# GpSimd's products with B issued three steps ahead of their scans in place of two, in a selective-scan kernel on one core

## The reference

```python
dt = softplus(einsum('blr,dr->bld', dt, dt_proj_w) + dt_proj_b)
A = -exp(A_log)
def step(h, inputs):
    dt_t, B_t, C_t, u_t = inputs
    dA = exp(dt_t[:, :, None] * A)
    h = dA * h + (dt_t * u_t)[:, :, None] * B_t[:, None, :]
    y = einsum('bdn,bn->bd', h, C_t)
    return (h, y)
...
y = ys.transpose(1, 0, 2) + u * D
y = y * silu(z)
```

## Time and profile before

| | us |
|---|---|
| median of 3 runs | 1285.89 |
| lowest, highest | 1283.64, 1287.6 |
| the profiled execution | 1284.42 |
| its span, first to last instruction | 1282.6 |

### The profile page before, as it was taken

How to read it: one execution, slowest core, us unless ns; L and a number is a source line. 1 busy time by engine, 2 the same in 40 slices (tenths; PEclk the granted TensorE clock), 3 DMA queues, 4 the chain that set the end, 5 groups by cost and what they waited for, 6 DMA issues and landing times.

```text
span 1282.6 us, 13041 instructions
## 1 busy us (share of the span) xinstructions
PE 1072.5 (84%) x3642; PEld 613.6 (48%) x3642; DVE 1150.1 (90%) x1341; ACT 819.0 (64%) x1532; POOL 1106.9 (86%) x747
## 2 busy tenths in 40 slices
PE   5678878888888887888888889888878878888797
PEld 4334545545545544544455455445445445454344
DVE  1299999999999999999999999999999999999782
ACT  2476766766666667757667666666667676576543
POOL 4199898898898898998988988988988989989663
PEclk8699998998998999999999989989999999998898
DMA  6222221221222312212222212222122132222561
GB/s 162 76 76 76 81 100 65 98 100 58 99 76 86 101 57 105 100 57 98 87 77 80 101 57 99 93 71 99 59 102 101 57 105 100 74 99 87 181 206 37
DMA packets 64538, 116.78 MB, mean 91 GB/s; under 512 B 34218, under 2 KB 47954, under 8 KB 64466
## 3 DMA queue, kind: packets, MB, share of 16 engines
q1 hardware_dynamic: 64466, 115.96, 26.9%
HBM read 108.47 MB, written 7.47 MB: 90 GB/s over the span
## 4 chain that ended last, share of the span: by engine, by line
POOL 27%; DVE 24%; issue 21%; PE 19%; ACT 7%; POOLq 0%; DMA 0%; DVEq 0%; SPq 0%; ACTq 0%
POOL SCAN L414 15%; DVE SCAN L984 15%; PE Yp L711 7%; POOL SCAN L426 6%; DVE SCAN L939 5%; PE PP L740 2%; PE PP L862 2%; PE PP L790 2%; PE PP L842 2%; POOL XN L451 2%; PE PP L835 1%; DVE GATES L968 1%; ACT SGZ L599 1%; POOL GATES L419 1%; POOL XN L442 1%
## 5 line engine op out<-in xcount | busy, mean ns | idle before, releaser
L984 DVE TENSOR_TENSOR_SCAN SCAN<-DA,CAR,SCAN 128x384 f32<-128x384 f32 x768 | 729.8, 1000 | 39.3 <-POOL SCAN L426 35.7
L414 POOL TENSOR_TENSOR SCAN<-SCAN,CS 128x768 f32<-128x768 f32 x384 | 692.3, 1817 | 23.1 <-DVE SCAN L984 18.9
L711 PE MATMUL Yp<-SCAN,IDENT 128*128 128x384 f32 x1536 | 592.6, 511 | 101.1 <-POOL SCAN L414 93.0
L491 ACT ACTIVATE DA<-UDT,A 128x384 f32<-128x384 f32 x768 | 441.6, 581 | 365.3 <-DVE SCAN L984 362.5
L711 PEld LDWEIGHTS Yp<-SCAN,IDENT 128*128 128x128 f32 x1536 | 288.8, 198 | 309.8 <-POOL SCAN L414 147.3
L939 DVE TENSOR_TENSOR SCAN<-UDT,BB 128x768 f32<-128x768 f32 x288 | 268.4, 932 | 11.1 <-PE BB L693 9.2
L426 POOL TENSOR_TENSOR SCAN<-UDT,BS 128x768 f32<-128x768 f32 x96 | 174.4, 1817 | 0.0
L862 PE MATMUL PP<-XN,WT 128*128 128x384 f32 x384 | 140.4, 501 | 0.0
L446 POOL TENSOR_TENSOR UDT<-UDT 128x768 f32<-128x768 f32 x24 | 43.5, 1811 | 69.9 <-DVE UDT L1068 69.9
L862 PEld LDWEIGHTS PP<-XN,WT 128*128 128x128 f32 x384 | 75.6, 199 | 56.7 <-issue 11.7
L693 PE MATMUL BB<-PT,SEL 96*128 96x384 bf16 x288 | 97.7, 340 | 4.1 <-DVE SCAN L939 4.1
(11 more groups left out here) (167 smaller groups left out, 1090.2 us busy)
## 6 DMA issues: line engine op xcount, KB each, us to landing
CS<-bc_rows SPq DMA_DIRECT2D x96, 768.0 KB, 4.1
BS<-bc_rows SPq DMA_DIRECT2D x24, 768.0 KB, 6.0
out<-XN SPq DMA_DIRECT2D x32, 192.0 KB, 2.5
X<-in_x SPq DMA_DIRECT2D x24, 192.0 KB, 3.5
X<-in_L_ffn_memory_tokens SPq DMA_DIRECT2D x16, 256.0 KB, 3.0
XN<-in_L_ffn_memory_tokens SPq DMA_DIRECT2D x16, 256.0 KB, 3.3
bc_rows<-XDT SPq DMA_DIRECT2D x24, 48.0 KB, 1.5
X<-in_L_ffn_memory_router SPq DMA_DIRECT2D x1, 512.0 KB, 4.0
```

Source lines behind the costliest of these rows:

```text
L414: pool.tensor_tensor(M[:, n1 % MRING], HB[:, n1 % HRING], over_halves(CS[:, n1 % CRING]), ALU.mult).then_inc(m_ready, 1)
L491: act.activation(DA[:, h, 0:T], DT[:, par, h], ACT.Exp, scale=A[:, h, n:n + 1])\
L711: last = pe.matmul(Yp[:, h, 0:T], IDENT[:, :], M[:, n3 % MRING, h], start=n3 == 0, stop=n3 == NS - 1)
L984: dve.tensor_tensor_scan(HB[:, s % HRING, h], DA[:, h, 0:T], HB[:, s % HRING, h], CAR[:, ds(J * NS * HALVES + s * HALVES + h, 1)], ALU.mul ...
```

## The change

GpSimd's `step` issues the product with B for state s + 3 where it issued it for state s + 2. The states 3, 5, 7 and 9 so get their product in the steps 0, 2, 4 and 6 in place of 1, 3, 5 and 7. The wait for `car_saved` follows n2 and stays what it was for each state.

```diff
--- before.py
+++ after.py
-                if main and s + 2 in POOL_STATES:
+                if main and s + 3 in POOL_STATES:
-
-                    n2 = s + 2
+
+                    n2 = s + 3
                     pool.wait_ge(bs_loaded, 16 * (J + 1))
                     pool.wait_ge(dtu_ready, J + 1)
                     pool.wait_ge(car_saved, 4 * BATCH + 4 * J + (n2 - HRING) // GRP + 1)
```

## The result

| | before | after |
|---|---|---|
| median, us | 1286.09 (4 runs, 1283.64 to 1287.6) | 1314.72 (4 runs, 1313.2 to 1317.12) |
| ratio to before | | 1.0226, interval 1.0202 to 1.025 |
| span of the profiled execution, us | 1282.6 | 1314.2 |

The change makes the kernel slower by 28.6 us, 2.3%. The direction was forecast; the forecast loss was 15.4 us, and the time lies 2.7 us above the forecast range.

The account below looks back on a forecast made before the run. No engine is full; a unit is bound by a ring of GpSimd from DTU to B(9) and VectorE from scan 9 to the next DT. 20 units x 0.72 plus 1 us gave +15.4, 1285.9 to 1301.3 us; range 1284 to 1312.

Parts of the forecast that it names:

- The waits for B go: VectorE's waits before scans 3, 5 and 9 for GpSimd's products with B all vanish: minus 1.76 us a unit.
- GZ, +1.39: GpSimd's GZ, one slot later, makes VectorE's VV, ahead of drive(4), U and scan 3, start 1.39 us later.
- BB(10) and the means, +0.72 together: On TensorE, M4 one slot later delays BB(10) and the means, so VectorE's scan 10 starts 0.72 us later each unit.
- M(10)'s wait: GpSimd's wait for scan 10 ahead of M(10) grows from 0.32 to about 1.0 us.
- No collision of the moved products with VectorE, and L968 as before: Large VectorE operations in steps 0 to 6 read PSUM, so moved products collide with nothing; L968 keeps its anchors.
- The step that failed: Later BB(6), BB(8) and output projection on TensorE fall into 1.7 us of room before M4; costed at nothing.
- Unit 0 loses nothing: The first unit has no GZ and no VV, so it was to lose nothing.
- The units 21 and 22: Fewer means or a VV that comes late anyway: 1 us of loss together, an estimate.
- The rival of the clock: TensorE's 1.2 GHz stretch reaches past M4, costing another 1.4 us a unit: 1315 us for half, 1329 for all; chance 0.09.
- TensorE catches up: Rival: the chain from Yp(4) has unseen cover, only GZ binds, minus 7.4 us, 1278.5 us; chance 0.10.
- the race at L968 turns: Rival: VectorE reaches L968 ahead of GpSimd's product in each unit, saving 1.56 us, 1270 us; chance 0.05.

Follow-up runs that it names:

- fill_both: The changed kernel with 17 unused matmuls on TensorE ahead of Yp(0) and 7 ahead of Yp(4); 1299.91 us, 1.0104 to before.
- a_fill: The changed kernel with 20 unused matmuls on TensorE ahead of Yp(0); 1317.81 us, 1.0255 to before.
- b3_back: The changed kernel with only B(3) put back to two steps ahead, where it was before; 1317.21 us, 1.0239 to before.
- v_b579: Kernel before with B(5), B(7), B(9) a step earlier; TensorE's means ahead of Yp(6), dt projection, BB(10) and D product ahead of Yp(4); 1297.89 us.
- b7_back: The changed kernel with only B(7) put back to two steps ahead, behind M(4); 1314.48 us, 1.0217 to before.
- b3_only: The kernel before with only B(3) moved to three steps ahead; 1315.15 us, 1.0224 to before.
- v_all: The changed kernel with TensorE's means ahead of Yp(6), and dt projection, BB(10) and product with D ahead of Yp(4); 1316.22 us, 1.0222 to before.
- v_pe: Kernel before, products with B unmoved; TensorE's means ahead of Yp(6), dt projection, BB(10) and product with D ahead of Yp(4); 1295.68 us, 1.007.
- b_fill: The kernel before with 12 unused matmuls on TensorE ahead of Yp(0); 1285.19 us, 1.0001 to before.

## Why the prediction was right in sign and short in size

- *The waits for B go*: right. No scan of the units 1 to 20 waits for L426.
- *GZ, +1.39*: right, 1.36 in the timeline, 25.8 us in 19 waits.
- *BB(10) and the means, +0.72 together*: right at full clock, and only there. `fill_both` shows drive(10) waiting 0.92 (0.75 forecast), XC 0.31 (0.35 to 0.45), scan 10 late by 0.73, a unit of 50.40, M(10)'s wait at 20.7 us in 20 (1.0 forecast) and 1299.91 us for 1301.3. In after itself none of these is the binding wait: drive(10) doesn't wait, drive(6) does.
- *No collision of the moved products with VectorE, and L968 as before*: right. M in steps 0 to 6 kept 1.8 us a piece, L968 its 2.5.
- *The step that failed*: "BB(6), BB(8) and the output projection then fall into the 1.7 us that TensorE has before M4 [...] I cost these at nothing; if that cover is gone, a late BB(6) costs some tenths, and drive(10)'s wait of 0.75 swallows them." The term was put at nothing, and it measured 1.16 us a unit. The working, from the rows: BB(6) had 2.22 us ahead of drive(6) before, 0.14 of which the start of drive(6) takes, and VectorE comes there 1.39 - 0.32 = 1.07 later, so BB(6) could be 3.15 us late for nothing. Yp(0) is 1.77 us later, which that cover holds. But from the start of Yp(0) to the end of BB(6) it is 5.81 us in after (576.96 to 582.77) against 3.19 in before (611.15 to 614.34), 2.62 more at the low clock: 4.39 late in all, 1.24 beyond the cover, and drive(6) waits 1.16. Yp(1) adds another 0.3. The 1.7 us ahead of M(4) were gone as well, and drive(10) had no wait left that could have swallowed the late BB(6). With the low clock a unit loses 1.51 us where the sum had 0.72: 0.79 a unit, 15.8 us over twenty units, against the 13.2 us by which the medians miss the forecast.
- *Unit 0 loses nothing*: not so. At the first operation behind L419 of unit 1 (GZ at 110.83 before, B(3) at 112.17 after) after is 1.3 us late, 0.4 of it from ahead of unit 0. The units 21 and 22 lost 1.1 us for a forecast of 1.
- *The rival of the clock* was named, with a price that came out near the result (1315 for half of the units), at 0.09 and for the wrong reason. That the number is near is luck. I let the clock count only if the low stretch reached past M(4), and held against it that the low stretches of before ended with the x projection. In after they reach into Yp(1) and no further; that is enough, because BB(6), which VectorE waits for, stands in them. I priced the steps behind the longer idle stretch with full-clock durations. The rows of the units 1 to 20 of before alone would not have given the loss either: Yp(0) or the x projection was slow in 12 of them, but the low clock added only 1.3 to 1.7 us a unit (2.93 and 1.71 us in unit 12), about half of the 3.2 us in after, and with that BB(6) comes out just in time on paper. The row that had it was the earlier trace rows, which I read only for the 0.14 us: it is BB(6) of unit 22 and drive(6) waiting 0.40 for it, behind 3.40 us of idle, a Yp(0) of 2.90 us and an x projection of 2.77. With these durations BB(6) comes out 1.1 us late.
- *Where the low clock did fall ahead of M(4)'s chain* is in `a_fill` and `b3_back`, about every second unit, for 1.7 us a unit there (52.09 against 50.38; the rival had 1.4).
- *TensorE catches up, and the race at L968 turns*: neither happened. The contention at L968 can grow, though, which I had not on my list (`v_b579`).

Why the mean unit comes out at 51.1 to 51.2 us both when every unit has a low Yp(0) (after, `b7_back`, `b3_only`, `v_all`) and when about every second one has a low Yp(4) (`a_fill`, `b3_back`: 51.24 and 51.14 over the units 1 to 20) is open. In the first four kernels it is hardly chance: their lists differ, the first units take 49.9 to 50.8 us, and all four grow to the same 51.20 as the low stretch grows. What makes it settle there no run shows.

## What to carry to other kernels

Where a change lengthens an idle stretch of TensorE, work out the matmuls behind it at both levels of the clock, for a low stretch longer than the measured one too, and see for each result that another engine waits for whether its cover still takes up the difference. An operation put ahead on a queue delays all that it passes, and the one that feeds an engine's first work of a unit is the dearest to pass: here one product ahead of GZ and M(0) made the whole loss, and B(5) and B(9), with TensorE's means put ahead of Yp(6), could move at a small gain (3 us, and 6 with the idle stretches filled). A matmul stretch filled with unused matmuls is a cheap experiment that tells clock from order, if each idle stretch that it uncovers is filled too. A reorder on TensorE itself can open such a stretch (`v_pe`).

## What the runs showed of the hardware that I had not expected

- Behind 4.54 us of idle TensorE runs at 1.2 GHz in each of the units 2 to 21 of after (Yp(0) at 2.92 or 2.93 us; the median matmul of the x projection took 847 ns, and 487 in before); behind 2.78 us it did so in 11 of the units 1 to 20 of before, in part or for all of Yp(0), and not in others; behind 1.95 us in about every second unit of `a_fill`. The Trainium skill, TensorE: Matmul & The Clock Gate, What's actually happening, has 1.2 GHz as the state after idling and 2.4 GHz as the one that activity releases; the rows agree with these two levels, and show that the same idle length can come out either way.
- How much later the low clock made the kernel depended on what waited behind it: not at all in before (`b_fill` at 1.0001), 14.8 us in after.
- VectorE's L968 was held for 4.58 us by GpSimd operations in a row, against 2.5 beside one and 0.96 when it came first.
